# High probabilities times high and low value weights in one product of 512 columns, and two additions a tile

## The reference

```python
def xattn(x, context, Wq, Wk, Wv, Wo, bo):          # H = 16, DH = 64, SCALE = DH ** -0.5
    q = (x @ Wq).reshape(b, n, H, DH)
    k = (context @ Wk * SCALE).reshape(b, m, H, DH)
    v = (context @ Wv).reshape(b, m, H, DH)
    attn = softmax(einsum('bihd,bjhd->bhij', q, k))
    return einsum('bhij,bjhd->bihd', attn, v).reshape(b, n, H * DH) @ Wo + bo

def ffn(h, gate_w, w1, b1, w2, b2):                 # combine: the two largest router shares
    for e in range(E):
        hmid = gelu(h @ w1[e] + b1[e])
        out = out + combine[:, e] * (hmid @ w2[e] + b2[e])
    return out

x = x + tanh(g_xattn[0]) * xattn(layernorm(x), ctx_1024, ...)
x = x + tanh(g_ffn[0]) * ffn(layernorm(x), ...)
```

## Time and profile before

| | us |
|---|---|
| median of 3 runs | 322.09 |
| lowest and highest run | 322.02 and 322.09 |
| the profiled execution | 321.86 |
| its span, first to last instruction | 319.8 |
| PE busy in the span | 314.9 |
| DVE busy | 233.9 |
| ACT busy | 164.1 |
| POOL busy | 78.7 |

### The profile page before, as it was taken

One profiled execution on the slowest core, in us unless ns is written; L12 is line 12 of the kernel. 1 busy time (PEld: TensorE's weight loads), 2 busy tenths in 40 slices (PEclk: granted clock), 3 DMA queues, 4 the chain that ended last, 5 costly groups with the idle time before them and its releaser, 6 DMA issues.

```text
span 319.8 us, 5745 instructions
## 1 busy us (share of the span) xinstructions
PE 314.9 (98%) x1881; PEld 272.6 (85%) x1881; DVE 233.9 (73%) x563; ACT 164.1 (51%) x577; POOL 78.7 (25%) x158
## 2 busy tenths in 40 slices
PE   8999999999999999999999999999999999999996
PEld 8978988989999999888788888888887899888896
DVE  1989997988889999999998475466767554442643
ACT  2658556686765768766366254444543442321320
POOL 1416548484465535425600000000000000000000
PEclk9999999999999999999999999999999999999999
DMA  7991000000000027500016250000020000000011
GB/s 275 382 162 6 1 2 0 2 1 3 0 0 3 0 83 251 196 1 0 2 8 255 78 186 1 0 0 0 22 101 11 2 0 2 0 0 0 2 65 66
DMA packets 20765, 17.35 MB, mean 54 GB/s; under 512 B 11068, under 2 KB 16900, under 8 KB 20612
## 3 DMA queue, kind: packets, MB, share of 16 engines
q1 hardware_dynamic: 20464, 16.51, 17.2%
q10 hardware_dynamic: 276, 0.52, 0.5%
HBM read 14.93 MB, written 2.10 MB: 53 GB/s over the span
## 4 chain that ended last, share of the span: by engine, by line
PE 88%; DVE 7%; DMA 2%; issue 1%; ACT 1%; SPq 0%; DVEq 0%
PE ps L1105 26%; PE ps L1106 26%; PE ps L1107 26%; PE ps L1190 4%; DMA xt<-in_x_dram 2%; PE ps L1279 1%; PE ps L1125 1%; DVE mx L857 1%; PE ps L1163 1%; DVE pT_lo L815 1%; PE ps L1221 1%; PE ps L1377 1%; ACT sx L587 1%; DVE stats L736 1%; DVE sm L826 1%
## 5 line engine op out<-in xcount | busy, mean ns | idle before, releaser
L674 ACT ACTIVATE gel<-ps,b1sel 128x512 f32<-128x512 f32 x64 | 43.9, 690 | 95.5 <-PE ps L1107 95.4
L1064 DVE CAST h_hi<-gel 128x512 fp32r<-128x512 f32 x64 | 28.4, 444 | 58.7 <-ACT gel L674 58.4
L587 ACT ACTIVATE sx<-ps,mx 128x64 f32<-128x64 f32 x128 | 38.3, 327 | 27.6 <-DVE mx L857 27.6
L1105 PE MATMUL ps<-yT_hi,w_hi 128*128 128x512 f32 (+1 forms) x128 | 50.5, 395 | 0.0
L1106 PE MATMUL ps<-yT_lo,w_hi 128*128 128x512 f32 (+1 forms) x128 | 50.0, 391 | 0.0
L1107 PE MATMUL ps<-yT_hi,w_lo 128*128 128x512 f32 (+1 forms) x128 | 49.9, 390 | 0.0
L1066 DVE TENSOR_TENSOR h_lo<-gel,h_hi 128x512 fp32r<-128x512 f32 x64 | 44.9, 702 | 2.2
L473 POOL TENSOR_TENSOR sx<-sx,rs 128x512 f32<-128x512 f32 x32 | 33.1, 1056 | 48.1 <-DVE rs L831 48.0
L1105 PE MATMUL ps<-h_hi,w_hi 128*128 128x512 f32 x96 | 38.4, 400 | 0.0
L1107 PE MATMUL ps<-h_hi,w_lo 128*128 128x512 f32 x96 | 37.5, 390 | 0.0
L1106 PE MATMUL ps<-h_lo,w_hi 128*128 128x512 f32 x96 | 37.4, 390 | 0.0
(11 more groups left out here) (145 smaller groups left out, 673.7 us busy)
## 6 DMA issues: line engine op xcount, KB each, us to landing
stage_w<-in_L_ffn_w_dram SPq DMA_DIRECT2D x7, 1024.0 KB, 7.4
out_dram<-xt SPq DMA_DIRECT2D x6, 256.0 KB, 2.5
wqT<-in_L_xattn_Wq_dram SPq DMA_DIRECT2D x2, 512.0 KB, 6.8
wv_sb<-in_L_xattn_Wv_dram SPq DMA_DIRECT2D x2, 512.0 KB, 8.4
wo_sb<-in_L_xattn_Wo_dram SPq DMA_DIRECT2D x1, 1024.0 KB, 13.6
xt<-in_x_dram SPq DMA_DIRECT2D x1, 1024.0 KB, 11.0
stage_w<-in_L_ffn_w_dram SPq DMA_DIRECT2D x2, 512.0 KB, 4.4
wk_sb<-in_L_xattn_Wk_dram ACTq DMA_DIRECT2D x1, 512.0 KB, 4.4
```

The lines of the kernel that those rows point to most:

```text
L587: last = nc.scalar.activation(sx[:, par, c0:c0 + M], ps[:, 2 * par + 1, c0 - BANK:c0 - BANK + M], ACT.Exp, bias=mx[:, par, h:h + 1], accum ...
L674: nc.scalar.activation(gel[:, f % 4, :], ps[:, h_bank, :], ACT.Gelu, bias=b1sel[:, b, slot, f:f + 1]).then_inc(gelu_done, 1)
L1064: nc.vector.tensor_copy(h_hi[:, f % 4, :], gel[:, f % 4, :]).then_inc(hhi_ready, 1)
L1105: mm(acc, hi_w, hi_x, start=start, stop=False)
```

## The change

The high probabilities of a block now stay in the array for one product of 512 columns (high and low value weights side by side), which fills the whole of bank 6. The low probabilities times the high value weights are a product of 256 columns into the left half. A block thus has two matmuls and two weight loads instead of three and three. In the last block the order is turned, so that the 512-column product ends the sum. The two halves of the bank are then partial sums of the same tile, and DVE adds both to `xt`: first the right half, then, after a wait on its own semaphore `x1_half`, the left half. As each tile now uses the whole bank, PE waits for `x1_done` of tile t-1 instead of t-2.

```diff
+        x1_half = sem("x1_half")
@@ residual
             def residual(t):
 
                 tile = xt[:, ds(t, 1), :].rearrange("p o d -> p (o d)")
-                q = t % 2
                 dve.wait_ge(out_done, t + 1)
-                nc.vector.tensor_tensor(tile, ps[:, 6, q * D:(q + 1) * D], tile, ALU.add).then_inc(x1_done, 1)
+                nc.vector.tensor_tensor(tile, ps[:, 6, D:2 * D], tile, ALU.add).then_inc(x1_half, 1)
+                dve.wait_ge(x1_half, t + 1)
+                nc.vector.tensor_tensor(tile, ps[:, 6, 0:D], tile, ALU.add).then_inc(x1_done, 1)
@@ end of PE's step
-                    wait_pos(pe, x1_done, t - 1)
+                    wait_pos(pe, x1_done, t)
                     bm = (t // TB) * NP
-                    acc = ps[:, 6, par * D:(par + 1) * D]
                     for m in range(NP):
                         if m % 4 == 0:
                             pe.wait_ge(plo_ready, 2 * t + m // 4 + 1)
...
-                        vh, vl = (vw[:, ds(bm + m, 1), c * D:(c + 1) * D].rearrange("p o n -> p (o n)") for c in range(2))
-                        last = three(acc, pT_hi[:, par, m, :], pT_lo[:, par, m, :], vh, vl, m == 0, m == NP - 1)
-                    last.then_inc(out_done, 1)
+                        both, high = (vw[:, ds(bm + m, 1), 0:n].rearrange("p o n -> p (o n)") for n in (2 * D, D))
+                        if m < NP - 1:
+                            mm(ps[:, 6, :], pT_hi[:, par, m, :], both, start=(m == 0), stop=False)
+                            mm(ps[:, 6, 0:D], pT_lo[:, par, m, :], high, start=False, stop=False)
+                        else:
+                            mm(ps[:, 6, 0:D], pT_lo[:, par, m, :], high, start=False, stop=False)
+                            mm(ps[:, 6, :], pT_hi[:, par, m, :], both, start=False, stop=True).then_inc(out_done, 1)
```

## The result

The changed kernel takes 324.01 us (median of 6 runs, 323.76 to 324.29), the kernel before 322.09 (6 runs, 322.02 to 322.36). The ratio is 1.0059, 95% interval 1.0048 to 1.0070: slower by 1.9 us. The forecast was 325.1, the range 321.9 to 326.4.

The account below looks back on a forecast made before the run. PE was taken as the bound, with DVE a second bound just under it in the attention steps. Carried DVE delay 2.84 - 0.10 (PE's gain) + 0.31 (hidden rows) = 3.05 us slower, median 325.1 us, range 321.9 to 326.4.

Parts of the forecast that it names:

- What bounds the kernel: Attention steps: DVE, in a ring with ACT, is a second bound just under PE; ACT waits 27.6 us for DVE's maxima.
- PE's wait costs nothing: Before value products: waiting for tile t-1's residual is always met earlier than the wait for low probabilities, so no cost.
- DVE's addition, 0.45 us: DVE's residual: the second addition with its wait adds 0.45 us a tile, 7.2 us over 16 tiles; low end 0.34.
- The cover, tile by tile: DVE's idle time after each residual takes up part of the additions; 2.84 us of delay is carried to tile 15.
- PE's gain: Value products: 2.88 us a tile becomes 2.78, saving 0.10 us a tile, 1.6 us in all; only tile 15's kept.
- The hidden rows, 0.31 us: First hidden rows after tile 15: DVE is 3.29 us late there, so PE loses another 0.31 us.
- The signs in the profile: Changed profile: PE's first product of tile 2 near 45.5, of tile 15 near 138.7; a tile's products take 2.78 us.
- The sum: Whole kernel: 2.84 - 0.10 + 0.31 = 3.05 us slower, a median of 325.1 us.
- The smaller version of the walk: Same tile-by-tile sum with 0.34 us an addition: 1.8 us slower, median 323.9; given 0.15 of the forecast's 0.70.
- The first, that DVE's spare time covers the additions: Attention steps: DVE's idle time also swallows carried delay, PE's gain of 1.6 us remains, 320.5 us; chance 0.12.
- The second, cancelling: Attention steps: delay is lost in long idle times up to step 11, PE's gain offsets more; 321.5 to 322.7, chance 0.10.
- The third, that nothing is covered: Attention steps: idle times for ACT shrink, 15 x 0.45 = 6.75 us reaches PE, 328.5 us; chance 0.05 for above 326.4.

Follow-up runs that it names:

- Three additions: The changed kernel with the right half's addition made twice, each behind a wait for the one before: 329.44 us.
- none of the statistics: The kernel before, narrow products, without the statistics behind each residual: 321.49 us, ratio 0.9973 to 0.9992.
- one addition: The changed kernel with the right half's addition and its wait removed, 512- and 256-column products kept: 321.92 us.
- DVE relieved: Wide product, only one addition, no statistics behind the residual, against the narrow-product kernel without those statistics: 321.28 us beside 321.49.

## Why the prediction was right, and where not

**What bounds the kernel.** Right. DVE as the second bound, and the 27.6 us of the earlier trace rows as the sign that ACT moves with DVE, carried the whole forecast. Three additions and none of the statistics confirm it from both sides.

**PE's wait costs nothing.** Right, 322.13.

**DVE's addition, 0.45 us.** Right for the additions with the wait: 0.45 and 0.46 in the rows.

**The cover, tile by tile.** Right in which tiles have one, save tile 10, and too small in size: 2.84 us forecast, 2.17 measured. Up to tile 9 the errors are small or cancel (at tile 5 the cover was 0.20 and not 0.1, at tile 7 0.35 and not 0.52). The mis-sized term is the idle time that I took from the brackets. A bracket counts from the end of the row before, but DVE starts an instruction about 0.09 us before that end. At tile 9 the bracket says 0.25. The rows start 0.68 us apart where 0.34 is the unhindered distance, so the true cover is 0.34:

```profile
100.43 0.43 DVE L906 BATCH_NORM_STATS2 stats<-xt 128x6 f32<-128x256 f32 x1
...
107.50 0.43 DVE L906 BATCH_NORM_STATS2 stats<-xt 128x6 f32<-128x256 f32 x1
108.05 1.29 DVE L815 TENSOR_TENSOR pT_lo<-ps,pT_hi 128x512 fp32r<-128x512 f32 x2
```

At tile 10 (the two lower rows) there is no bracket at all, and still 0.55 us from start to start: a hidden cover of 0.21 where I had put none. By starts the leftovers are 0.15, 0.45, 0.45, 0.25, 0.10, 0.11, 0.24, -0.09, 0, 0.05 and 0.45 for tiles 0, 1, 3, 5, 7 and 9 to 14, together 2.16, against 2.17 measured. Two of them need a word. At tile 7 the idle time for PE covered 0.35 only, since PE was 0.96 late itself (the residual at 86.38 against 85.08, less the start) and DVE 1.31: 0.96 + 0.45 - 1.31 = 0.10. At tile 11 the cover ahead of the router's row is 0.42 by starts, and DVE had waited another 0.12 ahead of the residual. For the three additions covers taken in this way gave a walk of 7.2 us, those from brackets would have given 8.2, and the rows show 6.55.

**PE's gain.** The main sum was right to keep only tile 15's, 0.08 measured for 0.10. The gain of 1.6 us that the rivals used was wrong twice. A tile's products save 0.06 us in the stream, not 0.10, or 7.5 ns for each of 8 removed matmuls. And PE can't keep even those: in the profiles 0.17 us arrived with one addition, 0.41 with DVE relieved. The Trainium skill, TensorE: Matmul & The Clock Gate, section Back-to-back issue gap, gives an isolated gap of N / 2.4 + 2.5 ns, by which each would save 2.5 ns, an estimate. The rows decide for the larger number.

**The hidden rows, 0.31 us.** Right in kind, and by coincidence near in size. PE's lateness (start included) grew from 2.42 us behind tile 15's products (141.20 against 138.78) to 2.64 at the seventh hidden rows and stayed there to DVE's last row, so 0.22 us. DVE was late at the first of them by 2.38 instead of 3.29. Of the difference 0.67 came with the walk, and most of the rest from a low part of weights (line 986) that took 1.63 us before and 1.27 after.

**The signs in the profile.** Less the start PE's first product of tile 2 stands at 45.46, where 45.5 was forecast, and that of tile 15 at 138.00, where 138.7 was. A tile's products take 2.81 to 2.86 us and not 2.78.

**The sum.** Forecast +3.05, measured +2.36 in the profile and +1.92 in the medians: direction and mechanism right, size 1.1 us too large by the medians. 0.67 of it is the cover read from brackets. The remaining 0.44 is the difference between profile and medians. The profiled execution of the changed kernel was the slowest of its six, 0.28 above their median, and the start differs from profile to profile; this is not resolved further. The smaller version of the walk, with 0.34 for an addition, gave 323.9. It is close to the result by luck: an addition with its wait costs 0.45, and the covers were larger than either version had them.

**The rivals.** The first, that DVE's spare time covers the additions, is out, and its price of 320.5 was unreachable even without the second addition. The second, cancelling, is out: there was hardly anything to cancel with. The third, that nothing is covered, is out too: DVE was 2.17 us late at tile 15 and not 6.75.

## What to carry to other kernels

An engine's busy share over the whole span can hide a second bound. Take a window of the stage, follow the engine's list row by row, and measure its idle time from start to start. Then ask which of its idle times end with an engine that itself waits for it, since in this kernel these covered an addition once but never a delay that was carried. Idle time that ended with the main engine was the opposite: it swallowed carried delay, but not work put behind it. Trading eight small matmuls of PE for one DVE instruction a tile saved 0.06 us here and cost 0.45 where DVE had no cover, so such an exchange has to be priced on the receiving engine first.

## What the runs showed of the hardware

- Where nothing held it, a DVE instruction behind a row of 0.43 us started 0.34 us after that row's start, so about 0.09 us before its end. Waits below that show no bracket at all, and longer ones are understated by it (0.25 in the bracket at tile 9, 0.34 by starts).
- A dependent addition of 128x256 starts 0.45 us after the one before it, with a semaphore between them. One that doesn't depend on it and has no wait starts after 0.34 us.
- DVE and POOL rows are longer in some places where they meet. In the kernel before, POOL's multiplication at 136.62 took 1.60 us. It lay beside all but the start of DVE's row of line 979, and beside the first 0.55 us of the row of 1.63 us:

```profile
136.54 1.21 DVE L979 TENSOR_TENSOR w_lo<-stage_w,w_hi 128x1024 fp32r<-128x1024 f32 x1
136.62 1.60 POOL L492 TENSOR_TENSOR yb<-yb,rstd 128x256 f32<-128x256 f32 x1
137.67 1.63 DVE L986 SCALAR_TENSOR_TENSOR w_lo<-stage_w,swt,w_hi 128x1024 fp32r<-128x1024 f32 x1
```

In the changed kernel POOL's row has ended before the second of the two begins. POOL's takes 0.61 us there, and DVE's second row 1.27:

```profile
138.67 0.61 POOL L493 TENSOR_TENSOR yb<-yb,rstd 128x256 f32<-128x256 f32 x1
139.05 1.31 DVE L981 TENSOR_TENSOR w_lo<-stage_w,w_hi 128x1024 fp32r<-128x1024 f32 x1
140.29 1.27 DVE L988 SCALAR_TENSOR_TENSOR w_lo<-stage_w,swt,w_hi 128x1024 fp32r<-128x1024 f32 x1
```

That the overlap is the cause was not tested on its own, and spans on POOL are rough.
